# The second layer's keys and values, and the quantisation of the feed-forward weights, made in the experts' stage

## The chip, the cores and the metric

The kernel runs on one core of one Trainium2 chip. The metric is the device time of one execution in microseconds (us), the median of several runs.

## What is computed

Two layers with gates work on x, 64 sequences of 128 tokens by 256 numbers. Each layer has cross attention with 16 heads to a context (64 x 128 x 256), and then a feed-forward part. In the first layer that part is a mixture of 64 experts (each token goes to 8 of them, an expert takes 256 rows at most) with a shared expert. In the second it is a gated feed-forward with 704 inner columns whose activations and weights are quantised to 8 bits. Cut to what matters here:

```
for each layer L:
    q = norm(x) @ wq + bq;  k = ctx @ wk + bk;  v = ctx @ wv + bv      # ctx is the same in both layers
    x = x + tanh(g_xattn[L]) * (softmax(q k^T / 4, masked in L = 1) v @ wo + bo)
    x = x + tanh(g_ffn[L]) * ffn_L(norm(x))
ffn_0: route each token to 8 of 64 experts, silu(xe w1^T) * (xe w3^T) @ w2^T, weighted, added up; plus a shared expert
ffn_1: w_gate, w_up, w_down rounded to 127 steps of their rows' maxima; activations to 127 steps of one global maximum
```

Keys and values of the second layer depend on the context and the weights alone, not on what the first layer gives. So do the quantised weights.

## The kernel before

Each engine runs its own program, written out in full, and semaphores tie them. `phase_end` is a barrier of all five engines between stages. The stages are: constants; attention of layer 0 with routing and the shared expert (`attention_*(..., 0)`); the experts (`experts_*`); attention of layer 1 (`attention_*(..., 1)`); and two passes of the second feed-forward part.

**Slots.** A stage is a software pipeline. `slots` calls a `body` for slot s, and `stage(lag)` in it is batch (or expert) s - lag with its ring number, or nothing. In the attention of layer 1 the slot's letters are g = s + 1, f = s, m = s - 1, k = s - 2, o = s - 3, w = s - 4 and v = s - 5. Every engine works through its own body in order, so an instruction that waits holds all that stand behind it.

**A slot of layer 1.** TensorE: `scores(m)` into the four banks `tiles`, after mask matmuls (L336) that begin the same banks; `project_qk(f)` (L434) and `project_v(f)` (L449) from the context tile `cx`; masks and transposed scores `scores_t(k)` (L369); `heads_to_tokens(o)` (L480), `output(w)` (L469), `tokens_to_heads(o)` (L490), `transposes(g)` (L415), `maxima_t(m)` (L385), `values(k)` (L399). VectorE: `maximum(m)` (L810), `first_sum` of batch s + 2 (L852: the two halves `ax` of the first layer's result, loaded from the two accumulators in DRAM), `first_stats` (L862), `head_sums(o)` (L909), `head_norm(o)` (L918), `token_maximum`, `residual` (L835), statistics, `shifted(m)` (L822). ScalarE: two normalisations, `copy_qk(f)` (L621 queries, L624 keys in two masked forms), `copy_v(f)` (L634), the exponential (L601), three copies. The keys and values of the first three batches (`KV_FIRST`) are made at the end of the experts' stage, so those slots project queries alone.

**SyncE** issues the loads of layer 1 in `attention_sp`: in slot s, `load` for batch s + 3, first the context (L1090) after waits on the projections of four batches before, then the two `ax` loads (L1112) after a wait on `sum_done` of two batches before. The ring of `cx` has four tiles and that of `ax` two.

**Experts.** For each of 64 experts GpSimd gathers two blocks of 128 rows (L1442) two slots ahead and adds two blocks of results into an accumulator in DRAM (L1457); these are indirect DMAs. TensorE makes the map of rows (L1221), transposes the rows (L1234, ScalarE copies them, L1321), multiplies up (L1252) and down (L1270), and makes the router's logits (L1258). SyncE loads the weights of the expert four ahead.

**Quantisation.** `weights_dve` on VectorE, `weights_pe` and `weights_act` work at the end of the attention of layer 0, from about slot 61, in buffers that this stage no longer uses (`qkp`, `cxax`, `pt`). The main line L771 rounds one matrix of 128 x 1536. SyncE stores the result (L1504) behind the loads of the second layer's weights and the first experts' weights (L1180, L1181), and then ends the stage.

Of the kernel before, what the change touches and what calls it, by code (L numbers as in the profile page):

```python
# [5 lines left out]
def flamingo_gated_two_layers(nc: bass.Bass, a, out: bass.AP):  # L6
# [10 lines left out]
    P = 128  # L17
# [32 lines left out]
    KV_FIRST = 3  # L50
# [11 lines left out]
    hidden_away = nc.dram_tensor("hidden_away", [len(AWAY), P, IC * CT], f32).ap()  # L62
    ffn_int = nc.dram_tensor("ffn_int", [3, P, KC * IP], bf16).ap()

    ctx = ExitStack()
    with ctx:
# [147 lines left out]
        wraw = [qkp[:, 3 * n:3 * n + 3, :].rearrange("p a (c d) -> p (a c) d", d=D) for n in range(2)]  # L214
        wdraw = cxax[:, 0:6, :].rearrange("p a d -> p (a d)")[:, 0:KC * I].rearrange("p (k i) -> p k i", k=KC)
        wq_b = pt[1][:, 2:4, :].rearrange("p a d -> p (a d)").bitcast(bf16)[:, 0:KC * IP]
        ws = [w.rearrange("p a d -> p (a d)").bitcast(bf16)[:, 0:KC * IP] for w in (pt[0][:, 2:4, :], ovs[:, :, :], qkp[:, 0:2, :])]
# [78 lines left out]
        MADE_WEIGHTS = (8 if IREST else 6) * 2 + 11  # L296
# [26 lines left out]
        TILES_IN_0 = 8 * NB  # L323
# [3 lines left out]
        def attention_pe(pe, L):  # L327
            def sm(name):
                return f"{name}_{L}"

# [8 lines left out]
            def scores(m):  # L339
# [4 lines left out]
                wait(pe, sm("exp_done"), b - 1)  # L344
# [9 lines left out]
                last.then_inc(sem(sm("s_done")), 1)  # L354

            def scores_t(k):
# [4 lines left out]
                pe.wait_ge(sem(sm("max_done")), ahead(b, 2))  # L361
                if L == 1:
                    masks(1)
                pe.wait_ge(sem(sm("qm_done")), b + 1)
# [6 lines left out]
                last.then_inc(sem(sm("st_done")), 1)  # L371

            def maxima_t(m):
# [4 lines left out]
                pe.wait_ge(sem(sm("max_done")), b + 1)  # L378
# [6 lines left out]
                nc.tensor.transpose(bk[:, 0:P], mt[:, :], ident[:, :]).then_inc(sem(sm("mt_done")), 1)  # L385

            def values(k):
# [5 lines left out]
                pe.wait_ge(sem(sm("exp_done")), b + 1)  # L393
                pe.wait_ge(sem(sm("v_out")), b + 1)
                wait(pe, sm("at_out"), b)
# [5 lines left out]
                last.then_inc(sem(sm("pv_done")), 1)  # L401

            def transposes(f):
# [6 lines left out]
                if L == 0:  # L410
                    pe.wait_ge(sem(sm("v_out")), b + 1)
                else:
                    wait(pe, sm("v_out"), b)
# [4 lines left out]
            def project_qk(f):  # L418
# [5 lines left out]
                pe.wait_ge(sem(f"tile_in{r}"), (2 - L) * (4 * (b - r) + 16) + L * TILES_IN_0)  # L424
# [5 lines left out]
                for j in range(KC):  # L430
                    for n, w in enumerate((w_q, w_k)[:1 if L == 1 and b < KV_FIRST else 2]):
# [4 lines left out]
                last.then_inc(sem(sm("qk_done")), 1)  # L436
# [153 lines left out]
        def attention_act(act, L):  # L590
            def sm(name):
                return f"{name}_{L}"
# [1492 lines left out]
```

## Time and profile before

| | |
|---|---|
| median of 3 runs | 2064.66 us (2063.12 to 2065.77) |
| the profiled execution | 2069.3 us, its span 2067.5 us |
| TensorE matmul, busy | 1832.9 us, 89% |
| TensorE weight load | 1463.2 us, 71% |
| VectorE | 1402.3 us, 68% |
| ScalarE | 1119.8 us, 54% |
| GpSimd | 562.2 us, 27% |
| mean granted TensorE clock | 0.945 of 2.4 GHz |

The numbers are of one execution that the hardware profiler took. Times in the rows are us from the start of the span, unless they say ns. PE is TensorE's matmul and PEld its weight load, DVE is VectorE, ACT ScalarE, POOL GpSimd, SPq the queue of SyncE's DMA issues. `L434` is line 434 of the kernel. In a row of the timeline the first two numbers are start and duration, x16 are sixteen instructions merged, and brackets hold the idle time before it and what ended that. Ends of matmuls are modelled, and their durations overlap, so distances between starts are the surer figure.

### The profile page before, as it was taken

How to read it: one execution, taken by the hardware profiler on the slowest of the kernel's cores; microseconds unless marked ns; L12 is line 12 of the kernel's file. 1: busy time of each engine (PE TensorE's matmuls, PEld its weight loads, DVE VectorE, ACT ScalarE, POOL GpSimd, SP SyncE). 2: the span in 40 equal slices, each digit the busy share in tenths (PEclk: the TensorE clock that was granted, in tenths of full speed). 3: DMA queues.
4: the chain of work that ended last, by engine and by line, in shares of the span. 5: the costliest groups of instructions: out<-in, count | busy, mean ns of one | idle time of the engine just before them, and what ended most of it. 6: DMA issues, size and time to landing. Idle time of an engine off the chain costs nothing.

```text
span 2067.5 us, 55165 instructions
## 1 busy us (share of the span) xinstructions
PE 1832.9 (89%) x20966; PEld 1463.2 (71%) x20976; DVE 1402.3 (68%) x4715; ACT 1119.8 (54%) x2347; POOL 562.2 (27%) x551
## 2 busy tenths in 40 slices
PE   6999999999999994888778876999999999978855
PEld 4888888888888873666666664777777777753334
DVE  4778878787878776444444435666666666658988
ACT  3666666666666651111111124666666666658875
POOL 1000000000000001788888871111111111111147
PEclk9999999999999996888888888999999999999989
DMA  3122222222222215666666652111111111102355
GB/s 96 45 60 61 61 64 60 71 61 64 61 63 61 58 43 182 139 140 141 142 141 143 133 98 64 48 41 48 45 43 48 41 48 41 40 25 111 134 214 193
DMA packets 158646, 174.30 MB, mean 84 GB/s; under 512 B 22512, under 2 KB 142704, under 8 KB 156208
## 3 DMA queue, kind: packets, MB, share of 16 engines
q1 hardware_dynamic: 133568, 136.34, 21.9%
q0 software_dynamic: 24816, 34.42, 9.9%
q8 instruction: 170, 2.79, 0.6%
q14 instruction: 92, 0.75, 0.1%
HBM read 104.72 MB, written 65.98 MB: 83 GB/s over the span
## 4 chain that ended last, share of the span: by engine, by line
PE 66%; DVE 14%; issue 8%; POOL 5%; DMA 4%; ACT 2%; POOLq 0%; SPq 0%; DVEq 0%; ACTq 0%
PE bank L434 12%; PE tiles L369 7%; PE tiles L352 7%; PE bank L399 6%; PE bank L517 6%; PE bank L449 5%; PE bank L480 4%; PE bank L469 3%; PE bank L540 3%; PE tiles L1252 3%; DVE hmax L1660 2%; POOL accumulator L1457 2%; PE tiles L336 2%; POOL xr L1442 2%; DMA xr<-token_rows,tid 2%
## 5 line engine op out<-in xcount | busy, mean ns | idle before, releaser
L1920 POOL TENSOR_TENSOR rstd<-var,minus_half 128x2 f32<-128x2 f32 x138 | 96.1, 696 | 1142.9 <-DVE var L887 1142.7
L810 DVE TENSOR_REDUCE mt<-tiles 128x16 f32<-128x2048 f32 x128 | 293.5, 2293 | 113.6 <-PE tiles L352 113.6
L601 ACT ACTIVATE pt<-tiles 128x2048 f32<-128x2048 f32 x128 | 240.8, 1881 | 13.1 <-PE tiles L369 8.5
L1457 POOL DMA_INDIRECT accumulator<-ye,tid x128 | 205.0, 1601 | 42.8 <-issue 31.7
L624 ACT ACTIVATE qkp<-bank,kb,keep 128x128 f32<-128x128 f32 x500 | 205.2, 475 | 0.0
L1405 DVE TENSOR_SCALAR ye<-bank,wcol 128x256 f32<-128x256 f32 x128 | 56.0, 479 | 216.3 <-PE bank L1270 175.1
L434 PE MATMUL bank<-xt,w_q 128*128 128x128 f32 x1024 | 165.1, 285 | 0.9 <-ACT xt L609 0.9
L621 ACT ACTIVATE qkp<-bank,qb 128x128 f32<-128x128 f32 x256 | 96.0, 376 | 123.9 <-PE bank L434 123.7
L1442 POOL DMA_INDIRECT xr<-token_rows,tid x128 | 137.3, 1072 | 81.1 <-DVE within L1370 44.5
L434 PE MATMUL bank<-cxax,w_k 128*128 128x128 f32 x1000 | 154.3, 277 | 0.0
L434 PEld LDWEIGHTS bank<-xt,w_q 128*128 128x128 f32 x1024 | 136.8, 195 | 22.6 <-issue 20.9
L369 PE MATMUL tiles<-qm,qkp 32*128 32x128 f32 x4096 | 150.2, 283 | 1.4 <-DVE mt L810 1.4
L352 PE MATMUL tiles<-qkp 32*128 32x256 f32 x2048 | 148.1, 402 | 3.2 <-ACT qkp L624 3.2
L1321 ACT COPY xrt<-tiles 128x512 f32<-128x512 f32 x64 | 37.5, 586 | 206.6 <-PE tiles L1234 173.2
L369 PEld LDWEIGHTS tiles<-qm,qkp 32*128 32x128 f32 x4096 | 125.8, 186 | 27.2 <-issue 24.3
L399 PE MATMUL bank<-pt,vx 128*32 128x128 f32 x4096 | 138.4, 276 | 2.3 <-ACT pt L601 1.5
L434 PEld LDWEIGHTS bank<-cxax,w_k 128*128 128x128 f32 x1000 | 133.5, 194 | 0.0
L469 PE MATMUL bank<-w_o,at 128*128 128x256 f32 x512 | 131.8, 380 | 0.5 <-ACT at L676 0.5
L667 ACT COPY ovs<-bank 128x512 f32<-128x512 f32 x128 | 75.1, 587 | 102.2 <-PE bank L399 102.2
L449 PE MATMUL bank<-w_v,cxax 128*128 128x256 f32 x500 | 130.2, 383 | 0.0
L1234 PE MATMUL tiles<-ident,xr 128*128 128x128 f32 x256 | 53.0, 342 | 78.9 <-DMA xr<-token_rows,tid 78.9
L352 PEld LDWEIGHTS tiles<-qkp 32*128 32x128 f32 x2048 | 92.7, 185 | 34.9 <-issue 26.9
(255 smaller groups left out, 4079.3 us busy)
## 6 DMA issues: line engine op xcount, KB each, us to landing
cxax<-in_ctx SPq DMA_DIRECT2D x128, 128.0 KB, 2.6
cxax<-accumulator SPq DMA_DIRECT2D x128, 128.0 KB, 2.2
hidden_away<-h_ring SPq DMA_DIRECT2D x8, 1536.0 KB, 5.1
pt<-in_expert_up SPq DMA_DIRECT2D x36, 256.0 KB, 4.6
token_rows<-pay SPq DMA_DIRECT2D x64, 128.5 KB, 2.7
res<-in_x SPq DMA_DIRECT2D x64, 128.0 KB, 2.7
accumulator<-xa SPq DMA_DIRECT2D x64, 128.0 KB, 1.7
accumulator<-zt SPq DMA_DIRECT2D x64, 128.0 KB, 1.8
```

What stands on the lines that cost most here:

```text
L352: last = nc.tensor.matmul(both, qt[r % 2][rows, j, :], kp[r][rows, :, j, :], start=(L == 0), stop=True, skip_group_check=(L == 1))
L369: last = nc.tensor.matmul(tiles[:, i, n * P:(n + 1) * P], kp[r][rows, e, j, :], qm[rows, e, j, :], start=(L == 0), stop=True, skip_group_c ...
L399: last = nc.tensor.matmul(bank[7][32 * h:32 * h + 32, g * P:(g + 1) * P], vx[r][:, GH * g + h, :], pt[p][:, i, n * P:(n + 1) * P], start=T ...
L434: last = nc.tensor.matmul(o_, w[:, c, j * P:(j + 1) * P], (cx[r] if n else xt[p])[:, c, :], start=(c == 0), stop=(c == KC - 1))
L449: last = nc.tensor.matmul(bank[4][:, 0:D], cx[r][:, c, :], w_v[:, c, :], start=(c == 0), stop=(c == KC - 1))
L469: last = nc.tensor.matmul(bank[6][:, 0:D], at[r % 2][:, c, :], w_o[:, c, :], start=(L == 1 and c == 0), stop=(c == KC - 1))
L517: last = nc.tensor.matmul(bank[4][:, n * FS + j * P:n * FS + (j + 1) * P], w[:, c, j * P:(j + 1) * P], x2t[p][:, c, :], start=(c == 0), st ...
L601: nc.scalar.activation(pt[r % 2][:, :, :], tiles[:, :, :], ACT.Exp).then_inc(sem(sm("exp_done")), 1)
L624: last = nc.scalar.activation(kp[r][:, e, j, :], bank[5][:, (KC + j) * P:(KC + j + 1) * P], ACT.Identity, bias=kb[:, e, j:j + 1], scale=ke ...
L810: nc.vector.tensor_reduce(mt[:, :].rearrange("p (i n c) -> p i n c", i=RT, n=2 * KC)[:, :, :, 0], tiles[:, :, :].rearrange("p i (n k) -> p ...
L1442: nc.gpsimd.indirect_dma_start(out=xr[r][:, h, :], out_offset=None, in_=rows[:, :], in_offset=bass.IndirectOffsetOnAxis(ap=tid[n % 8][:, h ...
L1457: nc.gpsimd.indirect_dma_start(out=acc[p][:, :], out_offset=bass.IndirectOffsetOnAxis(ap=tid[b % 8][:, h:h + 1], axis=0), in_=ye[r][:, h, ...
```

## The change

Line numbers in front of functions are those of the kernel before. What it does:

- In the experts' stage TensorE gets `keys_or_values` between `rows_t` and `up`: for expert slot n, with n even, the keys of batches n and n + 1 (four matmuls of 256 columns), with n odd their values. ScalarE copies bank 5 to `kvs`, and SyncE stores it to a new DRAM tensor `keys_values` (256 KB for each slot). Pairs of context tiles are loaded four pairs ahead (`load_pair`). `rows_t` uses one PSUM bank in place of two.
- In the attention of layer 1 `project_v` and the key half of `project_qk` are gone, and so is the load of the context. `copy_qk` and `copy_v` read keys and values from `kvt`, a ring of two in SBUF. `load` fills it from `keys_values` with two DMAs, and these stand in front of the `ax` loads.
- `first_keys_values_*` and `KV_FIRST` are gone.
- The quantisation gets room of its own in rows 8 to 55 of `res` (free once batch 55 of the first layer is stored). Its loads, and the first four pairs of context, are issued in the slot of the first attention in which batch 56 is stored. VectorE does one step of it in each of the experts' slots from 3 on; TensorE transposes in slots 8, 9, 13, 14, 20, 21 and 23; SyncE stores the results in slots 11, 16 and 23.
- Semaphores of the two layers' attention are counted on over both (`first = L * NB`), which frees some of them and changes no wait otherwise.

```diff
@@ buffers
-        wraw = [qkp[:, 3 * n:3 * n + 3, :].rearrange("p a (c d) -> p (a c) d", d=D) for n in range(2)]
...
+        wraw = [room(8 + 6 * n, 6).rearrange("p (c d) -> p c d", d=D) for n in range(2)]
+        wdraw = room(20, 6)[:, 0:KC * I].rearrange("p (k i) -> p k i", k=KC)
+        wq_b = [room(26 + 3 * n, 3).bitcast(bf16)[:, 0:KC * IP] for n in range(3)]
+        ws = [room(35 + 3 * n, 3).bitcast(bf16)[:, 0:KC * IP] for n in range(3)]
+        cxp = [room(44 + 2 * k, 2).rearrange("p (c e t) -> p c e t", c=KC, e=2) for k in range(4)]
+        kvs = [room(52 + 2 * k, 2) for k in range(2)]
+        ROOM_FROM, ROOM_TO = 8, 56
+        kvt = [cxax[:, 2 * k:2 * k + 2, :].rearrange("p a d -> p (a d)") for k in range(2)]
@@ attention_pe, body of layer 1
                     project_qk(f)
-                    project_v(f)
                     scores_t(k)
@@ attention_act, copy_qk and copy_v
+                if L == 1:
+                    act.wait_ge(sem(f"kv_in{p}"), 16 * (b - p) + 32)
...
+                    k = bank[5][:, (KC + j) * P:(KC + j + 1) * P] if L == 0 else kvt[p][:, j * P:(j + 1) * P]
+                    for e in range(2):
+                        last = nc.scalar.activation(kp[r][:, e, j, :], k, ACT.Identity, bias=kb[:, e, j:j + 1], scale=keep[:, e:e + 1])
...
+                v = bank[4][:, 0:D] if L == 0 else kvt[p][:, D:2 * D]
@@ attention_sp, load
-                if L == 0 or b >= KV_FIRST:
-                    wait(sp, sm("v_done"), b - 3)
-                    wait(sp, sm("qk_done"), b - 3)
+                if L == 0:
+                    wait(sp, "v_done", first + b - 3)
+                    wait(sp, "qk_done", first + b - 3)
                     load_context(sp, b, r)
-                if L == 0:
                     sp.dma_start(res[:, bass.ds(b, 1), :].rearrange("p o d -> p (o d)"),
...
                 else:
+                    wait(sp, sm("qk_out"), 2 * (b - 1))
+                    wait(sp, sm("v_out"), b - 1)
+                    sp.dma_start(kvt[p][:, 0:D].rearrange("p (c t) -> p c t", c=KC),
+                                 keys_values[b - p].rearrange("p (c e t) -> p c e t", c=KC, e=2)[:, :, p, :]).then_inc(sem(f"kv_in{p}"), 16)
+                    sp.dma_start(kvt[p][:, D:2 * D], keys_values[b - p + 1][:, p * D:(p + 1) * D]).then_inc(sem(f"kv_in{p}"), 16)
                     wait(sp, sm("sum_done"), b - 1)
                     for n_ in range(2):
                         sp.dma_start(ax[p][:, n_, :], acc[n_][bass.ds(b * P, P), :]).then_inc(sem(f"ax_in{p}"), 16)
@@ attention_sp, body of layer 0
-                    if stage(5) is not None and stage(5)[0] == NB - 2:
+                    if stage(5) is not None and stage(5)[0] == ROOM_TO:
                         ffn_weights_in(sp)
@@ experts_sp
+            def keep_pair(e):
+                if e is None:
+                    return
+                n, r = e
+                p = r % 2
+                sp.wait_ge(sem("kv_out"), n + 1)
+                sp.dma_start(keys_values[n], kvs[p]).then_inc(sem(f"kv_kept{p}"), 16)
+                if p == 1 and n // 2 + 4 < PAIRS:
+                    load_pair(sp, n // 2 + 4)
+
             def body(stage):
                 load_weights(stage(0))
+                keep_pair(stage(1))
+                if stage(0) is not None and stage(0)[0] in WEIGHTS_OUT_AT:
+                    ffn_weights_out(sp, WEIGHTS_OUT_AT[stage(0)[0]])
@@ experts_pe
+            def keys_or_values(e):
+                if e is None:
+                    return
+                n, _ = e
+                j = n // 2
+                if n == 0:
+                    pe.wait_ge(sem("w_in"), 16 * 16)
+                pe.wait_ge(sem(f"pair_in{j % 4}"), 8 * (j - j % 4) + 32)
+                wait(pe, "kv_out", n)
+                for k in range(2):
+                    for c in range(KC):
+                        if n % 2 == 0:
+                            weights_, moving = w_k[:, c, k * P:(k + 1) * P], cxp[j % 4][:, c, :, :].rearrange("p e t -> p (e t)")
+                        else:
+                            weights_, moving = cxp[j % 4][:, c, k, :], w_v[:, c, :]
+                        last = nc.tensor.matmul(bank[5][:, k * D:(k + 1) * D], weights_, moving, start=(c == 0), stop=(c == KC - 1))
+                last.then_inc(sem("kv_done"), 1)
@@ experts_act
+            def copy_pair(e):
...
+                act.wait_ge(sem("kv_done"), n + 1)
+                wait(act, f"kv_kept{p}", 8 * (n - p))
+                nc.scalar.copy(kvs[p], bank[5][:, :]).then_inc(sem("kv_out"), 1)
@@ experts_dve, body
                 hidden(stage(1))
+                if stage(0) is not None and stage(0)[0] > 2 and stage(0)[0] != E // 4 and stage(0)[0] != E // 4 + 4:
+                    next(weights, None)
                 next_layer(stage(0))
@@ the program of SyncE
             sp.wait_ge(sem("pv_done"), NB)
             first_expert_weights(sp)
-            ffn_weights_out(sp)
```

## Rows read from the trace of the kernel before

**Rows 1.** Busy time by stage: stretch, its length, each engine's busy, PEclk, DMA share, GB/s
```profile
749.00:809.00 60.00, 32.80 (x312) 26.01 (x310) 47.35 (x196) 16.56 (x34) 2.07 (x3) 0.79 0.45 145
809.00:1246.00 437.00, 344.57 (x1705) 281.83 (x1705) 191.65 (x873) 78.36 (x207) 342.24 (x256) 0.83 0.65 132
1246.00:1850.00 604.00, 578.66 (x9230) 435.82 (x9230) 398.43 (x893) 397.77 (x814) 94.04 (x132) 0.99 0.15 45
```

**Rows 2.** Timeline, one slot of the second attention: start, duration, engine, line
```profile
1502.94 0.71 PE L434 MATMUL bank<-xt,w_q 128*128 128x128 f32 x4
1503.08 2.29 DVE L810 TENSOR_REDUCE mt<-tiles 128x16 f32<-128x2048 f32 x1 [1.04 <-PE tiles L352]
...
1505.03 0.37 ACT L621 ACTIVATE qkp<-bank,qb 128x128 f32<-128x128 f32 x1 [1.82 <-PE bank L434]
1505.29 0.41 DVE L852 TENSOR_TENSOR res<-cxax 128x256 f32<-128x256 f32 x1
...
1505.79 0.43 PE L336 MATMUL tiles<-mask_bias,identb 32*32 32x512 bf16 x16
...
1506.92 0.40 ACT L634 COPY vx<-bank 128x256 f32<-128x256 f32 x1
...
1507.75 1.03 PE L469 MATMUL bank<-w_o,at 128*128 128x256 f32 x4
1508.24 0.42 DVE L918 TENSOR_TENSOR on<-bank,rden 128x256 f32<-128x256 f32 x1
...
1508.72 0.44 PE L490 MATMUL bank<-ident,on 128*128 128x128 f32 x2
...
1510.77 0.43 PE L336 MATMUL tiles<-mask_bias,identb 32*32 32x512 bf16 x16
...
1512.21 0.71 PE L434 MATMUL bank<-xt,w_q 128*128 128x128 f32 x4
```

**Rows 3.** Timeline, the stage's end: mask matmuls of slots without projections
```profile
1835.40 0.43 PE L336 MATMUL tiles<-mask_bias,identb 32*32 32x512 bf16 x16
...
1844.32 0.43 PE L336 MATMUL tiles<-mask_bias,identb 32*32 32x512 bf16 x16
```

**Rows 4.** Timeline, the stage's first loads and the sum that waits for them
```profile
1246.43 3.91 SPq L1112 DMA_DIRECT2D cxax<-accumulator  x6
1249.09 0.42 DVE L852 TENSOR_TENSOR res<-cxax 128x256 f32<-128x256 f32 x1 [14.86 <-DMA cxax<-accumulator]
```

**Rows 5.** Timeline, the first slots, with queries alone: at the low clock, then the full
```profile
1253.43 2.08 PE L434 MATMUL bank<-xt,w_q 128*128 128x128 f32 x8 [0.46 <-ACT xt L609]
...
1255.86 0.65 PE L336 MATMUL tiles<-mask_bias,identb 32*32 32x512 bf16 x16
...
1258.12 1.16 PE L434 MATMUL bank<-xt,w_q 128*128 128x128 f32 x8
...
1259.32 0.63 ACT L621 ACTIVATE qkp<-bank,qb 128x128 f32<-128x128 f32 x2 [2.28 <-PE bank L434]
```

**Rows 6.** Busy time in the experts' stage: a gap of TensorE, and what follows
```profile
1028.10:1031.00 2.90, 0.00 (x0) 0.00 (x0) 2.74 (x14) 0.00 (x0) 2.29 (x3) 0.66 0.72 205
1031.00:1036.00 5.00, 4.96 (x17) 4.25 (x17) 0.10 (x1) 0.97 (x2) 4.08 (x4) 0.51 0.56 93
```

**Rows 7.** Timeline, the first attention's end: quantisation and SyncE's last issues
```profile
782.12 1.75 DVE L761 TENSOR_REDUCE s_gu<-qkp 128x6 f32<-128x1536 f32 x1
...
790.61 0.96 DVE L771 TENSOR_SCALAR qkp<-qkp 128x1536 f32<-128x1536 f32 x1
...
802.14 0.43 SPq L1181 DMA_DIRECT2D xt<-in_L_ffn_w  x1
...
809.13 1.79 SPq L1844 DMA_DIRECT2D res<-in_mask_1x1xSxS_ik  x4
```

**Rows 8.** GpSimd's indirect DMAs, one line each: ns min/median/max, first and last start
```profile
L1442 POOL DMA_INDIRECT xr<-token_rows,tid x128: 1012/1061/1157, 812.8 to 1218.1; - x128
L1457 POOL DMA_INDIRECT accumulator<-ye,tid x128: 1557/1592/1851, 831.2 to 1238.0; - x128
```

## Prediction of the time

> **What bounds the kernel now.** I read the busy times by stage first. There are four stages that matter here: the first layer's attention with routing up to 749 us, its tail to 809, the experts to 1246, the second attention to 1850 [rows 1]. The change touches the last three. In the second attention TensorE is busy 579 of 604 us, VectorE and ScalarE two thirds of it: the reader would say that TensorE is the bound and that taking matmuls away pays one for one. In the experts' stage the figures to see are TensorE's 345 of 437 us at a granted clock of 0.83 and the DMA share of 0.65.
>
> The second view is one slot of the second attention in order of time [rows 2]. A slot is 9.27 us (L434 at 1502.94 and again at 1512.21). Inside it one group of PSUM banks, `tiles`, is written by the scores, read by the maximum (L810, 2.29 us), written again by the transposed scores, and read by the exponential. Of L434 and L449, the projections of queries, keys and values, all but the queries leave; they run while the maximum runs. So their time is not the slot's time. The trace has slots without any projection, at the end of the stage: from mask matmul to mask matmul 8.92 us [rows 3]. That is the floor that the change can reach with everything else as it is: 0.35 us less per slot, although it takes 1.77 us of matmuls away (the eight key matmuls about 0.9, the values 0.87; L469, of the same form as the values, is 1.03 with its overlap).
>
> **Second attention: what is put in.** Eight matmuls of keys and four of values go, and with them one load of context in each slot. In come two loads, of keys and of values, into two buffers (`kvt`), each read by ScalarE in the place of PSUM (the same count of activations, priced the same). What matters is the order on SyncE. In `load`, batch b's key and value loads wait for `qk_out_1` and `v_out_1` of batch b-2, since there are two buffers. Behind them, in the same queue, stand the two loads of the accumulators (`ax`) of batch b. Before, `ax` stood behind a wait on batch b-4's projection, so two slots early. VectorE needs `ax` of batch b in `first_sum`, right behind the maximum, in slot b-2: the very slot in which ScalarE copies the values of batch b-2. Everything behind `first_sum` on VectorE waits with it: `head_sums`, `head_norm`, the residual, the shifted queries. For `head_norm` waits TensorE (L490), in order, and behind that stand the values' matmuls and the next slot's scores, whose projection ScalarE's next copy waits for. It is a closed loop of one slot.
>
> I walk it from L434 = 0, with the distances of [rows 2], and of other rows where the slot changes:
> - queries alone to ScalarE's first copy: 1.20 (1258.12 to 1259.32, where only queries are projected [rows 5]), in place of 2.09
> - ScalarE's first copy to the end of the copy of values (1505.03 to 1507.32): 2.29, together 3.49
> - two issues for keys and values at 0.43 and a small gap [rows 7]: 0.95, together 4.44
> - first issue of `ax` to `first_sum`: 2.66 (1246.43 to 1249.09, where the DMA alone sets it [rows 4]), together 7.10; before it starts at 2.35
> - `first_sum` and `first_stats` 0.85, reciprocal and `head_norm` 0.71 (L918 ends at 1508.66): together 8.66
> - `head_norm`'s end to the next mask matmul (1510.77): 2.11, and to the next L434 (1512.21) 1.44: **12.21 us** for a slot, 2.94 more.
>
> **The clock.** In this new slot TensorE ends L469 about 5.5 us after L434 (the maximum ends at 2.43, then 3.0 of work as from 1505.79 to 1508.78 [rows 2]) and waits for L490 till 8.7: 3.2 us idle in every slot. Before there is no such gap and the clock is 0.99 [rows 1]. What a gap of that length does stands in the experts' stage: 2.9 us without a matmul, the clock falls to 0.5 and the next 5 us run at 0.51, the 1.2 GHz level [rows 6]. Five gaps of 2.6 to 3.1 us between 1028 and 1100 all show it, with 2.5 to 5 us of work at the low level behind each; of two gaps of 2.2 (at 1008) and 2.3 us (at 1837) the first does, for 7.9. What it costs on the path: full queries 2.08 against 1.16, and mask to queries 2.26 (1255.86 to 1258.12) against 1.44 [rows 2, 5]. All of the path after the gap at the low level is 0.8 + 0.9 + about 1.3 for the maxima's transpose and the values + 0.7 where L490 and L415 outgrow VectorE's cover, 3.7 us. I take 4.4 us of the low level after a gap, the mean of those six, half of it lost: 2.2. **Slot 14.4 us**, between 12.2 and 15.9.
>
> Slots 3 to 61 pay it (batches 2 to 63 are loaded this way): 59 x 5.1 = 303. The three first slots are short now, and pay about 3 each; the first `ax` starts 0.9 behind two new issues. Sum **+313** for the stage.
>
> **Tail of the first stage.** The quantisation ran on VectorE there, and its last store is what SyncE waits for: the experts' stage begins at 809.13. Without it SyncE's last issue is the expert weights' at 802.14, and these come about 1.8 us earlier, since L761 and its small steps (782.12, 1.75 us and more) no longer stand between routing steps. **-8 us**, bounds -6 to -10 [rows 7]. The weights' 5 loads and 8 of context now come in one slot of the first attention: 13 issues at 0.47 are 6 us on a queue that has about 7 issues in a slot of 11.6 us, and the next user of each buffer is two slots away. I take 0; it could be 3.
>
> **Experts' stage.** Here GpSimd makes the descriptors: 2 x 1.06 and 2 x 1.59 us and four gaps of 0.3, 6.5 us for each of 64 experts, 437 us in all [rows 1, 8]. It is the bound. TensorE gets 64 x 0.87 us (four matmuls of 256 columns): 345 + 56 is 401, up to 61 more at the granted clock, 406 of 437: it fits, and its gaps get shorter, which speaks for a higher clock. ScalarE gets 64 copies of 512 columns and VectorE some 17 us in 20 slots, at 192 of 437: cover enough. The DMA engines are the tight one: 384 KB more per expert is 58 GB/s beside 132, at the row's own ratio 0.28 more share, 0.93. Each gather, each add and each weight load still has a slot or more of slack. I take **+4**, with 0 and +25 as ends (the upper is a tenth of a slot per expert with one stalled slot in five). If the cover were gone, TensorE's part is worth 56 us.
>
> The quantisation's `tensor_scalar` of 1536 elements takes 0.96 us [rows 7], beside GpSimd's descriptors in the new place; gathers vary by 0.1 and adds by 0.3 us about their medians [rows 8], with short VectorE work beside them. The Trainium skill (SBUF — State Buffer, "Who interferes with whom") says that VectorE's single-input SBUF operations in their two-port mode and GpSimd lock each other out of a shared port pair for a whole instruction. By that rule, which speaks against this move, six such operations would delay the bound engine by at most 5.7 us; the sum above takes nothing for it and its upper end holds it.
>
> **Sum.** -8 + 4 + 313 = +309. The profiled execution took 2069.3 us (span 2067.5), so it becomes 2378; it lies 4.6 above the median of the runs, and for the median I say **2374**.
>
> **Rivals.**
> - The loop closes, but the clock stays up: slots of 12.2 us, 59 x 2.94 = 173, and 10 - 8 + 4: 2244. For it: one gap of 2.3 us did no harm. Against: five of five over 2.6 did.
> - The loop closes and all the path runs at the low level: 59 x 6.6 = 390, in all +396: 2461. For it: the fall comes anew in every slot. Against: no work behind a gap stayed low for over 8 us.
> - The experts' stage turns to TensorE or DMA: a tenth longer, +45 in place of +4: 2415. For it the share of 0.93; against, that the added work shortens the idle time that lowers the clock.
> - Faster: the `ax` loads land before VectorE needs them. Then TensorE's projections are gone, slots fall to the floor of 8.92, 62 x 0.35 = 22, and with -8 and +4 the time is 2039. It decides at `first_sum` starting less than 2.4 us after L434, that is if `ax` could be issued ahead of the copies of batch b-2. The order of the queue says that it can't.
>
> **How the numbers follow.** Forecast 0.53, full clock 0.20, low clock 0.09, longer experts' stage 0.11, faster 0.06, and 0.01 for no change. The range reaches from a little below the full-clock case to a little above the low one, 2225 to 2470, which leaves about 0.15 out. A measurement of this kernel tells a change from none at about 0.2%. Faster 0.06, same 0.01, slower 0.93.
>
> **What would show it.** After the change `first_sum` (the sum of the two `ax` halves) waits for a DMA in each slot of the second attention, some 3.5 to 5 us; TensorE's longest idle is ahead of the transposes of `on` and is put down to VectorE; the stage's slots are 12 to 16 us and its clock 0.75 to 0.9. The experts' stage keeps 6.4 to 6.6 us per expert and GpSimd has next to no idle time. The experts begin near 801. If slots are at 9 us or less, the queue argument is wrong; if GpSimd waits for `ye` or for its own adds, the experts' term is.

## The result, and the profile after the change

The changed kernel takes 2378.88 us (median of four runs, 2372.41 to 2381.23), the kernel before 2065.22 us in the same comparison: a ratio of 1.150 (95% interval 1.148 to 1.152). The prediction was 2374. The profiled execution took 2380.58 us, its span 2378.8.

| | before | after | difference | predicted |
|---|---|---|---|---|
| the experts' first gather | 812.8 | 800.6 | -12.2 | -8 |
| from there to the second attention's first load | 433.6 | 443.8 | +10.1 | +4 |
| from there to the first maximum over all tokens | 612.5 | 927.9 | +315.4 | +313 |
| the rest | 208.5 | 206.6 | -1.9 | 0 |

Busy time of the changed kernel by stage, to be laid beside [rows 1] (stretch, its length; busy time of PE, PEld, DVE, ACT and POOL; granted clock, DMA share, GB/s): the tail of the first attention, the experts, the second attention.

```profile
737.00:797.00 60.00, 35.20 (x365) 29.06 (x364) 33.68 (x188) 16.89 (x40) 2.75 (x4) 0.85 0.25 77
797.00:1244.00 447.00, 399.19 (x2219) 336.84 (x2218) 209.17 (x900) 115.22 (x262) 347.64 (x256) 0.96 0.81 187
1244.00:2172.00 928.00, 581.55 (x8512) 410.56 (x8512) 402.63 (x910) 423.18 (x832) 95.27 (x134) 0.85 0.13 39
```

In the second attention TensorE was busy in 96% of the time before and is in 63% now, at a clock of 0.85. No other engine has taken its place: VectorE and ScalarE are under 46%, DMA at 0.13. A stage in which nobody is busy is bound by a chain of waits. The costliest groups name it (busy, mean ns | idle before, releaser):

```profile
L497 PE MATMUL bank<-ident,on 128*128 128x128 f32 x256 | 65.8, 345 | 233.2 <-DVE on L933 233.2
L867 DVE TENSOR_TENSOR res<-cxax 128x256 f32<-128x256 f32 x64 | 27.2, 425 | 355.6 <-DMA cxax<-accumulator 355.6
L688 ACT COPY at<-bank 128x256 f32<-128x256 f32 x128 | 47.6, 372 | 316.7 <-PE bank L497 316.7
```

ScalarE (L688) waits for TensorE (L497), TensorE for VectorE (L933), and VectorE for a DMA: `first_sum` (now L867) waits 355.6 us for `ax`, 5.6 in each of 63 slots. One slot shows where that DMA was (start, duration, engine, line, idle time before it and what ended that):

```profile
1512.61 1.20 PE L444 MATMUL bank<-xt,w_q 128*128 128x128 f32 x8
...
1513.85 0.37 ACT L630 ACTIVATE qkp<-bank,qb 128x128 f32<-128x128 f32 x1 [2.13 <-PE bank L444]
...
1515.89 0.40 ACT L647 COPY vx<-cxax 128x256 f32<-128x256 f32 x1
1516.36 0.52 SPq L1122 DMA_DIRECT2D cxax<-keys_values  x1
...
1516.93 0.80 SPq L1124 DMA_DIRECT2D cxax<-keys_values  x1
...
1517.78 0.91 SPq L1127 DMA_DIRECT2D cxax<-accumulator  x2
1520.69 0.42 DVE L867 TENSOR_TENSOR res<-cxax 128x256 f32<-128x256 f32 x1 [5.65 <-DMA cxax<-accumulator]
...
1521.77 0.42 DVE L933 TENSOR_TENSOR on<-bank,rden 128x256 f32<-128x256 f32 x1
...
1522.24 0.44 PE L497 MATMUL bank<-ident,on 128*128 128x128 f32 x2 [4.15 <-DVE on L933]
...
1523.43 1.94 PE L408 MATMUL bank<-pt,vx 128*32 128x128 f32 x32
...
1525.29 0.65 PE L345 MATMUL tiles<-mask_bias,identb 32*32 32x512 bf16 x16
...
1527.17 0.60 PE L444 MATMUL bank<-xt,w_q 128*128 128x128 f32 x3
```

The copy of the values (L647) ends at 1516.29, and SyncE issues the next key load (L1122) at 1516.36: it stood waiting for that copy. The `ax` loads (L1127) come third, at 1517.78, and land when VectorE has waited 5.65 us. The group of projections starts 14.56 us apart here. As a mean over 61 slots (from the third `first_sum` to the last) a slot takes 9.14 us before and 14.13 after; the medians are 9.27 and 14.15, since the first slots are short in both.

### The profile page after: what moved, and what is told of

Read it like the earlier page. It is cut to its first block, busy times and chain, and to the rows that moved or that the text cites. A ratio compares the mean times of both kernels' runs of the same rounds, so it can differ in the third digit from the quotient of the medians.

```text
span 2378.8 us, 55048 instructions
## 1 busy us (share of the span) xinstructions
PE 1876.1 (79%) x20710; PEld 1483.4 (62%) x20720; DVE 1400.3 (59%) x4713; ACT 1174.4 (49%) x2411; POOL 567.2 (24%) x551
## 3 DMA queue, kind: packets, MB, share of 16 engines
q8 instruction: 168, 2.75, 0.5%
## 4 chain that ended last, share of the span: by engine, by line
PE 57%; DVE 13%; DMA 10%; ACT 7%; issue 6%; SPq 5%; POOL 2%; POOLq 0%; ACTq 0%; DVEq 0%
PE bank L444 8%; PE bank L408 7%; PE tiles L361 6%; DMA cxax<-accumulator 6%; PE bank L524 5%; ACT qkp L633 4%; PE tiles L378 3%; DMA xr<-token_rows,tid 3%; PE bank L1268 3%; PE tiles L1300 2%; PE bank L476 2%; PE bank L547 2%; PE bank L456 2%; PE bank L497 2%; DVE hmax L1709 2%
## 5 line engine op out<-in xcount | busy, mean ns | idle before, releaser
L497 PE MATMUL bank<-ident,on 128*128 128x128 f32 x256 | 65.8, 345 | 233.2 <-DVE on L933 233.2
L867 DVE TENSOR_TENSOR res<-cxax 128x256 f32<-128x256 f32 x64 | 27.2, 425 | 355.6 <-DMA cxax<-accumulator 355.6
L688 ACT COPY at<-bank 128x256 f32<-128x256 f32 x128 | 47.6, 372 | 316.7 <-PE bank L497 316.7
L497 PEld LDWEIGHTS bank<-ident,on 128*128 128x128 f32 x256 | 29.0, 159 | 266.3 <-DVE on L933 258.7
L408 PE MATMUL bank<-pt,vx 128*32 128x128 f32 x4096 | 188.4, 342 | 1.8 <-ACT pt L608 1.2
L361 PE MATMUL tiles<-qkp 32*128 32x256 f32 x2048 | 166.5, 442 | 3.6 <-ACT qkp L633 3.5
L444 PE MATMUL bank<-xt,w_q 128*128 128x128 f32 x1024 | 155.7, 286 | 0.9 <-ACT xt L616 0.9
L408 PEld LDWEIGHTS bank<-pt,vx 128*32 128x32 f32 x4096 | 138.3, 137 | 28.2 <-issue 15.1
L345 PE MATMUL tiles<-mask_bias,identb 32*32 32x512 bf16 x2048 | 64.8, 456 | 86.5 <-DVE mt L825 86.5
L361 PEld LDWEIGHTS tiles<-qkp 32*128 32x128 f32 x2048 | 103.5, 209 | 46.3 <-issue 34.8
```

Source lines behind the costliest of these rows:

```text
L361: last = nc.tensor.matmul(both, qt[r % 2][rows, j, :], kp[r][rows, :, j, :], start=(L == 0), stop=True, skip_group_check=(L == 1))
L408: last = nc.tensor.matmul(bank[7][32 * h:32 * h + 32, g * P:(g + 1) * P], vx[r][:, GH * g + h, :], pt[p][:, i, n * P:(n + 1) * P], start=T ...
L444: last = nc.tensor.matmul(o_, w[:, c, j * P:(j + 1) * P], (cx[r] if n else xt[p])[:, c, :], start=(c == 0), stop=(c == KC - 1))
L497: last = nc.tensor.transpose(bank[7][:, c * P:(c + 1) * P], on[r % 2][:, c * P:(c + 1) * P], ident[:, :])
```

## The experiments

My theory is the prediction's: the slot is a closed loop from ScalarE's copies over SyncE's queue to `first_sum` in the same slot, and the clock falls in the gap that this makes. "Slot" below is the mean that was just defined. Where a time has no interval beside it, it is that of a single run; the four runs of the changed kernel lie within 9 us of each other.

**The order in SyncE's queue.** The two accumulator loads moved in front:

```diff
+                    wait(sp, sm("sum_done"), b - 1)
+                    for n_ in range(2):
+                        sp.dma_start(ax[p][:, n_, :], acc[n_][bass.ds(b * P, P), :])...
                     wait(sp, sm("qk_out"), 2 * (b - 1))
                     wait(sp, sm("v_out"), b - 1)
...
-                    wait(sp, sm("sum_done"), b - 1)
-                    for n_ in range(2):
-                        sp.dma_start(ax[p][:, n_, :], acc[n_][bass.ds(b * P, P), :])...
```

> Only the order of the four loads of a slot in the second attention is changed: the two accumulator loads stand in front of the two of keys and values, with the same waits. Theory (the accumulator loads are held behind the copies of keys and values): first_sum waits for nothing, slots fall from 14.1 us to the floor of 8.9 that the kernel before shows without projections, TensorE's gap of 4.2 us goes and with it the low clock; 62 x 5.2 = 322 less, about 2055 us. Rival (the two added loads cost by themselves, their traffic or SyncE's time): the slots stay above 12 us and the time above 2250. Rival (TensorE is still the bound and all of the projections' 1.77 us comes off): slots of 7.5 us, 1970.

Measured: 2050.54 us, a ratio to the kernel before of 0.993 (0.990 to 0.995). A slot takes 8.86 us, the granted clock is 1.00 in the middle of the stage and the waits of `first_sum` for DMA shrink from 355.6 to 16.1 us. In a slot of it `first_sum` starts 2.35 us after the projection, and waits for nothing:

```profile
1504.65 1.16 PE L444 MATMUL bank<-xt,w_q 128*128 128x128 f32 x8
...
1507.00 0.41 DVE L867 TENSOR_TENSOR res<-cxax 128x256 f32<-128x256 f32 x1
...
1507.14 0.44 PE L345 MATMUL tiles<-mask_bias,identb 32*32 32x512 bf16 x16 [1.33 <-DVE mt L825]
```

No transfer and no instruction was taken away, so neither the added loads nor ScalarE's reads from SBUF cost the 328 us: their place in the queue did.

The same from the other side: the order stays, but the ring for keys and values has four tiles.

```diff
-        kvt = [cxax[:, 2 * k:2 * k + 2, :]... for k in range(2)]
+        kvt = [cxax[:, 2 * k:2 * k + 2, :]... for k in range(2)] + [w[:, :, :]... for w in (w_k, w_v)]
-                    wait(sp, sm("qk_out"), 2 * (b - 1))
-                    wait(sp, sm("v_out"), b - 1)
+                    wait(sp, sm("qk_out"), 2 * (b - 3))
+                    wait(sp, sm("v_out"), b - 3)
```

(`kvt` and its semaphores are then counted by the ring of four.)

> The changed kernel, order of SyncE's queue untouched (keys and values still in front of the accumulators' loads), but the ring for keys and values has four tiles in place of two (the other two are the weights w_k and w_v, idle in this stage), so their loads wait for the copies of four batches before. If the wait on the copies of two batches before closes the loop, it is open here too: slots of 8.9 us and a total as with the accumulators' loads in front, 2050 +-8. If instead it is the position of two more issues ahead of the accumulators' loads that costs, slots stay above 13 us and the total above 2300.

Measured: 2050.55 us, 0.992 (0.990 to 0.994), a slot of 8.80. So the accumulators' loads may stand third in the queue, if what stands in front of them needn't wait. It is the wait in front of the loads, for a copy of two batches before in a ring of two, that closes the loop.

What an issue in front of them costs, with the loop closed: the values' load is taken away (and ScalarE's waits count one load for each batch in place of two), so this kernel leaves out the values of the second layer.

```diff
-                    sp.dma_start(kvt[p][:, D:2 * D], keys_values[b - p + 1]...)
```

> The changed kernel without the load of the values in the second attention (the values read there are old data; the rest is done in full). Theory (each issue that stands in front of the accumulator loads is in the loop): one issue of 0.6 us and its gap off each slot, 13.5 in place of 14.1, 62 x 0.65 = 40 less, 2340. Rival (the wait for the copies is all of it, issues overlap): 2380. Rival (the loads' traffic delays the accumulators' landing): over 1 us a slot, below 2315.

Measured: 2355.62 us, a slot of 13.73: 0.40 less in each, 23 in all, where the issue and its gap are 0.65. At the median the first `ax` issue follows the copy of the values after 0.65 us in place of 1.28, and the sum follows that issue after 2.89 in place of 2.81. So the loop runs through the issues, and the slot keeps part of each one's price.

**The clock.** Filler matmuls between the output projection and the transposes of `on`, in every slot, twelve and then six:

```diff
+                    if o is not None and f is not None:
+                        pe.wait_ge(sem(sm("qk_out")), 2 * (f[0] + 1))
+                    for n_ in range(12 if o is not None and f is not None else 0):
+                        nc.tensor.matmul(bank[5][:, D:2 * D], w_k[:, n_ % 2, 0:P], w_v[:, n_ % 2, :], start=True, stop=True)
```

> The changed kernel with twelve matmuls of 256 columns more in each slot (2.6 us, results unused), where TensorE waits for head_norm, so that the gap of 4.2 us shrinks below 2. The loop through the loads is as before. Theory (a loop of some 13.1 us and 1 to 1.5 us more by the low clock): the clock of the stage goes from 0.86 to 0.97 or more, a slot from 14.1 to 12.9 to 13.1 us, the time down by 60 to 75 us to about 2310, although work was added. Rival (the clock costs nothing, the loop alone sets 14.1): no change, 2380. Rival (the added matmuls lie on the path): 2.6 us more in each slot, 2540.

Measured: 2369.77 us, a slot of 13.70. The size was wrong: such a matmul is recorded as two and takes about 0.45 us, where I had taken 0.22, so the twelve ran 5.3 us and ended about 1 us after `on` was there. The clock in the middle of the stage was 1.00, and most of the gain went into the overshoot. So this run gives no price; the next one does.

> As the kernel with twelve filler matmuls, but with six in each slot (about 2.6 us), so that they end before the normalised heads are there. It prices the clock: the same loop with TensorE kept busy. By my prediction's step the low clock costs 2.2 us in each slot, so 60 slots give 130 less: about 2250. By the reading of the slots after the change (two stretches of the path grew by 1.0 and 0.4 us against the full clock) it costs 1.0 to 1.4: slots of 13.0, 60 to 85 less in all, 2295 to 2320. If the clock costs nothing: 2380.

Measured: 2328.18 us, 51 less than the changed kernel; the slot 13.14, at a clock of 0.98 in the middle of the stage (0.86 in the changed kernel). One slot of it:

```profile
1503.43 1.16 PE L444 MATMUL bank<-xt,w_q 128*128 128x128 f32 x8
...
1504.63 0.37 ACT L634 ACTIVATE qkp<-bank,qb 128x128 f32<-128x128 f32 x1 [0.93 <-PE bank L444]
...
1506.68 0.39 ACT L651 COPY vx<-cxax 128x256 f32<-128x256 f32 x1
...
1508.36 0.91 SPq L1131 DMA_DIRECT2D cxax<-accumulator  x2
...
1508.75 2.75 PE L591 MATMUL bank<-w_v,w_k 128*128 128x256 f32 x12
1511.28 0.42 DVE L871 TENSOR_TENSOR res<-cxax 128x256 f32<-128x256 f32 x1 [5.41 <-DMA cxax<-accumulator]
...
1512.35 0.42 DVE L937 TENSOR_TENSOR on<-bank,rden 128x256 f32<-128x256 f32 x1
...
1512.83 0.44 PE L497 MATMUL bank<-ident,on 128*128 128x128 f32 x2 [1.33 <-DVE on L937]
...
1514.88 0.43 PE L345 MATMUL tiles<-mask_bias,identb 32*32 32x512 bf16 x16
...
1516.32 0.94 PE L444 MATMUL bank<-xt,w_q 128*128 128x128 f32 x6
```

At the full level the loop takes 12.89 us here (1503.43 to 1516.32; the median of all slots is 12.98). `first_sum` still waits 5.41. The low level costs 1.0 us of the mean slot (14.13 against 13.14), not 2.2, and 1.2 of the median one. The cost falls where the gap has just ended: from `on` to the masks 2.11 us here, 3.10 in the changed kernel, and from there to the projection 1.44 against 1.88.

**The experts' stage.** I measure it from the start of the first gather to that of the last add, both on GpSimd: 425.2 and 424.8 us in the two kernels with the old stage, 432.7 to 435.3 (mean 433.8) in nine with the new one, so +8.8. First, the three products and the three roundings of the quantisation cut to an eighth of their columns (most of each weight matrix is left unrounded):

```diff
-                st.then(V.tensor_tensor(wraw[n], wraw[n], inv[...].unsqueeze(2).broadcast_to([P, IC, D]), ALU.mult))
+                st.then(V.tensor_tensor(wraw[n][:, :, 0:32], wraw[n][:, :, 0:32], inv[...].unsqueeze(2).broadcast_to([P, IC, 32]), ALU.mult))
```

> The changed kernel with six of VectorE's quantisation instructions (the three products and the three roundings) cut to an eighth of their columns, so that the weights are quantised for a part only; count and order of instructions are unchanged. Theory (these instructions hold GpSimd, whose gathers of 1.06 us took 2.2 to 2.5 beside the products): the longest gather falls from 2.54 to under 1.3 us, the experts' stage shortens by 4 to 6 us of its 447.5. Rival (the stage is 10 us longer than before because of TensorE and DMA): it stays within 1 us.

Measured: a stretch of 430.2 us, 3.6 under that mean and 5.1 under the changed kernel; the total, 2382.61, doesn't show it, since the experts began at 807.6 there and at 800.6 in the changed kernel, which scatters. The trace of the changed kernel shows how VectorE's work reaches GpSimd:

```profile
840.40 1.75 DVE L777 TENSOR_TENSOR res<-res,inv 128x1536 f32<-128x1536 f32 x1
840.84 2.24 POOL L1481 DMA_INDIRECT xr<-token_rows,tid  x1 [0.31 <-issue]
...
845.31 2.15 POOL L1496 DMA_INDIRECT accumulator<-ye,tid  x1 [0.30 <-issue]
846.42 0.95 DVE L779 TENSOR_SCALAR res<-res 128x1536 f32<-128x1536 f32 x1
...
L1481 POOL DMA_INDIRECT xr<-token_rows,tid x128: 1007/1060/2538, 800.6 to 1215.6; - x128
L1496 POOL DMA_INDIRECT accumulator<-ye,tid x128: 1557/1598/2147, 822.5 to 1235.8; - x128
```

A gather takes 1.06 us at the median and 2.24 beside the product. The three products, each with both inputs in SBUF, lengthen three gathers by 1.2, 1.5 and 1.3 us; single-input operations of the quantisation lengthen three of the five adds that they meet by 0.35 to 0.55 us. Before, the longest gather was 1.16 us [rows 8]. With the cut, the longest gather and add take 1.75 and 1.73; that gather stands beside L781, a single-input operation which the cut leaves whole.

Second, the new transfers cut to an eighth. This kernel leaves out most of the keys and values, and its second attention loads parts of the context of the same size in their place:

```diff
-                sp.dma_start(keys_values[n], kvs[p]).then_inc(...)
+                sp.dma_start(keys_values[n][:, 0:64], kvs[p][:, 0:64]).then_inc(...)
-                sp.dma_start(cxp[j % 4][:, :, e, :], a["ctx_1024"]...)
+                sp.dma_start(cxp[j % 4][:, :, e, 0:16], a["ctx_1024"][..., 0:16]...)
```

> The changed kernel, with the new transfers of the experts' stage cut to an eighth (an eighth of each pair of contexts loaded, an eighth of keys and values stored), as many DMAs, matmuls and copies as there; the second attention loads parts of the context of the same size in place of its keys and values. From the first gather to the end of the last add: 427 us before, 437 after, 432 with the quantisation cut. If traffic is what is left of the 10 us, the stretch is 432 here too; if it is in the descriptors' own time and in the fill, it stays at 436 to 437. The DMA share falls from 0.86 to about 0.7 in either case, and the total is within 6 us of the changed kernel's.

Measured: the stretch 432.3 us at a DMA share of 0.72 in place of 0.85. That is 1.5 under the mean of the nine, and hardly outside their spread, so traffic is little of the 8.8, if any. The total was 2354.55, 24 less, which I had not expected: the slot of the second attention is 13.74. The two loads read the context there, in another layout, and their issues take 0.38 and 0.47 us at the median and not 0.52 and 0.60; the first `ax` issue follows the copy after 1.01 us in place of 1.28, and the sum follows it after 2.74 in place of 2.81. By the medians that is 0.34 of the 0.4 us that a slot lost.

GpSimd's own times split the 10.1 us between the two profiled kernels. Its gathers and adds last 342.2 us before [rows 1] and 347.6 after (the second row by stage above), 5.4 more, and 343.3 with the quantisation cut. Its idle times of over 0.6 us sum to 7.8 us before and 12.6 after, and these 4.7 are the rest; the short gaps between its instructions are 76.6 us in both.

Most of that rest stands at the stage's start. From first gather to first add it takes 18.4 us in the kernel before (18.6 in the other one with the old stage) and 21.9 in the changed one, and 21.1 to 22.4 in ten others with the new stage, the two cuts among them. In the changed kernel these stand before the first down projection (L1318), and L1268 is new:

```profile
805.86 3.62 PE L1268 MATMUL bank<-res,w_k 128*128 128x256 f32 x8
...
810.25 1.96 PE L1268 MATMUL bank<-w_v,res 128*128 128x256 f32 x8
812.05 1.89 PE L1300 MATMUL tiles<-xrt,wlast 128*128 128x256 f32 x8
...
815.36 1.89 PE L1268 MATMUL bank<-res,w_k 128*128 128x256 f32 x8
...
819.63 1.11 PE L1318 MATMUL bank<-wlast,he 128*128 128x256 f32 x4
```

While the pipeline fills, TensorE's work is the path, and three groups of the new matmuls are in it. That this is the cause of the 3.5 us is read, not tried.

**What taking the projections out is worth.** With the loop open the slot fell by 0.3 us only, though 1.77 us of matmuls had gone. In the kernel with the accumulators' loads in front TensorE waits 1.33 us for the maximum. Two work items moved into that wait:

```diff
                     project_qk(f)
-                    scores_t(k)
                     heads_to_tokens(o)
                     output(w)
+                    scores_t(k)
```

> The kernel with the accumulators' loads in front, and TensorE's order in the second attention changed: the transposes of the raw heads and the output projection stand before the transposed scores, in the 1.33 us in which TensorE waits for the maximum. If TensorE is still the bound there, the slot loses that wait whole: 7.6 us, 1970. If the loop through the banks of the scores holds it (scores 1.6, maximum 2.3, transposed scores 1.6, exponential 1.9, and the values' matmuls 1.1 behind it, in order), the slot is 8.6: about 0.3 less, 2030 +-8.

Measured: 2052.78 us (0.993, 0.991 to 0.995), nothing gained, a slot of 8.80. The wait for the maximum is gone, and TensorE waits 1.38 us ahead of the values' matmuls instead:

```profile
1508.11 1.88 ACT L608 ACTIVATE pt<-tiles 128x2048 f32<-128x2048 f32 x1 [0.45 <-PE tiles L378]
...
1509.88 0.37 ACT L688 COPY at<-bank 128x256 f32<-128x256 f32 x1
...
1510.40 1.08 PE L408 MATMUL bank<-pt,vx 128*32 128x128 f32 x32 [1.38 <-ACT at L688]
1511.41 0.43 PE L345 MATMUL tiles<-mask_bias,identb 32*32 32x512 bf16 x16
```

Neither expectation was right to the number: I had left out that the values' matmuls write a bank that ScalarE reads first (L688), and that this copy stands behind the exponential. So the values' matmuls moved out of the loop, behind the next slot's scores (`output` stands behind the transposed scores again):

```diff
                     # TensorE, against the kernel with the accumulators' loads in front
+                    values(o)
                     project_qk(f)
+                    heads_to_tokens(o)
                     scores_t(k)
-                    heads_to_tokens(o)
                     output(w)
                     tokens_to_heads(o)
                     transposes(g)
                     maxima_t(m)
-                    values(k)
                     # ScalarE
+                    copy_ov(o)
                     copy_qk(f)
-                    copy_v(f)
                     exponent(k)
+                    copy_v(f)
                     copy_at(o)
                     copy_xt(g)
-                    copy_ov(k)
```

> As the last, with the values' matmuls of a batch moved behind the next slot's scores (and ScalarE's copy of their result with them, its copy of the loaded values behind the exponential), so that they run during the maximum and not between the exponential and the next scores. If the loop through the banks of the scores is what holds the slot, it becomes 7.6 to 7.9 us, so 60 x 1.0 to 1.3 less than with the accumulators' loads in front alone: 1975 to 1995. If ScalarE (7.3 us of work in a slot) or a chain through it takes over: 8.3 to 8.9, 2015 to 2050.

Measured: 1984.36 us, 0.961 (0.959 to 0.962), a slot of 7.82. The loop through the banks of the scores was what held it. The same two orders in the kernel before, where the projections stay (ScalarE's copy of the values keeps its place ahead of the exponential there, since the next transposes need its bank; in this one point the orders differ):

```diff
                     # TensorE
+                    values(o)
                     project_qk(f)
                     project_v(f)
+                    heads_to_tokens(o)
                     scores_t(k)
-                    heads_to_tokens(o)
...
-                    values(k)
                     # ScalarE
+                    copy_ov(o)
...
-                    copy_ov(k)
```

> The kernel before (all projections in the second attention), with the same two reorderings of that stage as in the run with the values' matmuls behind the next scores. It tells what taking the projections out is worth once the loop through the banks of the scores is short. With TensorE's whole work in a slot (7.6 us there, and 1.77 of keys and values) it can't fall under 9.3 us, what it has: 2060 to 2075, no gain. If the reordering alone brought the 66 us, and the projections were still hidden, it would come near 1995.

Measured: 2069.50 us, 1.000 (0.999 to 1.002), a slot of 9.13. The orders alone bring nothing, the change with its queue mended brings 0.7%, and both together 3.9%. Last, both with four buffers as well, that is, the edits of the runs with `ax` in front, with four tiles and with the values late in one kernel:

> The kernel with the values' matmuls late, and four buffers for keys and values as well. In the former first_sum still waits 0.9 to 1.1 us in 53 slots for its loads, since they queue on SyncE behind the wait for the copy of values, which now comes after the exponential. If that wait holds the slot (7.62 us), it becomes 7.4 or so, and the total 1968 to 1978. If TensorE holds it (377 of 400 us busy there), the wait was beside it: 1984 +-4.

Measured: 1970.07 us, 0.952 (0.950 to 0.954): the fastest. The slot is 7.57; `first_sum`, which still waited for DMA 53 times with two buffers (73.8 us), does so once, at the stage's start:

```profile
1506.86 0.42 DVE L867 TENSOR_TENSOR res<-cxax 128x256 f32<-128x256 f32 x1
1507.05 0.14 PEld L345 LDWEIGHTS tiles<-mask_bias,identb 32*32 32x32 bf16 x16 [0.16 <-DVE mt L825]
...
1507.31 0.79 SPq L1122 DMA_DIRECT2D cxax<-accumulator  x2
...
1508.78 1.86 ACT L608 ACTIVATE pt<-tiles 128x2048 f32<-128x2048 f32 x1
...
1510.69 0.14 PEld L345 LDWEIGHTS tiles<-mask_bias,identb 32*32 32x32 bf16 x16 [0.26 <-ACT pt L608]
```

The slot is full: the next masks follow 1.9 us after the exponential's start (1508.78), TensorE's waits shown are 0.2 and 0.3 us, and it is busy in 384 of the 400 us from 1300 on. Against the kernel before with the same orders it is 99 us less, 1.56 in each slot: nearly the 1.77 us of matmuls one for one.

## Why the prediction was right, point by point

- **The closed loop** is shown from both sides: open it by the order or by two more buffers, and 328 us go. It was read off the order of one queue and the lengths of two rings.
- **Its length at the full level** was 12.21; it is 12.89. The copies end 0.15 later, mostly since two of ScalarE's key copies take 0.87 us from SBUF and took 0.80 to 0.82 from PSUM, as two rows of the kernel before show, in the slot of [rows 2]:

```profile
1505.30 0.80 ACT L624 ACTIVATE qkp<-bank,kb,keep 128x128 f32<-128x128 f32 x2
...
1506.23 0.82 ACT L624 ACTIVATE qkp<-bank,kb,keep 128x128 f32<-128x128 f32 x2
```

  The two issues and their gaps take 1.29 and not 0.95: I had priced them at 0.43, from a load of weights [rows 7], and these take 0.52 and 0.60. From the first `ax` issue to the sum it is 2.92, not 2.66. With -0.07 for the rest that makes 0.68. The wait of `first_sum` was accordingly 5.6 us a slot, above the 3.5 to 5 that I had named as its sign, and TensorE's gap 3.9 at the median and not 3.2.
- **The clock** I had at 2.2 us a slot; it costs 1.0 to 1.2. I had taken half of 4.4 us of low level as lost. Its length was about right: a clock of 0.86 in slots of 14.15 us is an estimate of 4.0 us at half the clock in each. Wrong was the half, which was about a quarter; I read that the rest lay beside VectorE's part of the loop or in the wait for the maximum, and no run separates the two. The two errors, +0.7 and -1.0, nearly cancelled: slot 14.4 predicted and 14.13 found. That 313 was met so closely is therefore in part luck. By place the sum fits: 304 of the 315 us lie between the third and the last `first_sum`, where I had 303, and 10 before the third, where I had 10. The clock of 0.85 in the stage lies inside the 0.75 to 0.9 named.
- **The experts' beginning**: -8 predicted, -12.2 in the profiled pair. Over all profiles (eleven at 800.6 to 807.6, mean 804.0, and two at 812.8 and 813.2) it is -9.1.
- **The experts' stage**: +4 predicted, within 0 to 25, and +8.8 to +10 found. GpSimd stays the bound (6.56 us an expert from the first add to the last, within the 6.4 to 6.6 named) and TensorE fits. The DMA share became 0.81, where I had worked out 0.93. But two terms were mis-sized. The new matmuls: four of 256 columns are eight in the trace, and cost 127 us and not 56 in all (66.7 and 60.6 for L1268); I read the +3.5 at the stage's start as their part. And I took nothing for what VectorE does to GpSimd's descriptors, where it is 3.6 to 5. The Trainium skill (SBUF — State Buffer, "Who interferes with whom") gives more than the one rule that I weighed: it says too that a VectorE instruction with both inputs in SBUF contends with a GpSimd instruction that reads SBUF. The trace agrees, and that half was the dearer one: 1.2 to 1.5 us for each of three gathers beside a product, against 0.35 to 0.55 for three adds beside a single-input operation.
- **The rivals.** Full clock (2244) falls: even held up by fillers the kernel takes 2328, since the loop itself was longer. All low (2461) and a longer experts' stage (2415) fall by the profile. The faster one decided at the point it named: with `ax` issued ahead, 2050.5 where I had worked out 2039.
- **The floor** of 8.92 us a slot, from the stage's last slots [rows 3], was right for the given order (8.86 and 8.80). It was a floor of the order and not of the work: 7.57 with another.

## What to carry to other kernels

Where a DMA queue serves two consumers, ask of each load what its wait is for and who stands behind it: here a wait on a copy of the same slot, put ahead of loads that had been two slots early, cost 15%, and either a swap of two blocks or two more buffers takes all of that back. Work taken off a busy engine is worth its time only if no loop through shared banks is as long: 1.77 us of matmuls brought 0.3 us, until one consumer was moved out of that loop, and then 1.3, and 1.56 with four buffers as well. Check the order of the work and the removal of work together, since here neither alone brought more than 0.8%, and both 4.8%.

## What the runs showed of the hardware that I had not expected

- A float32 matmul of the program is two matmuls in the trace, of 0.22 us each at 256 columns: twelve of the program ran 5.3 us, six 2.75.
- GpSimd's gathers lasted up to 2.54 us, 2.4 times their median, beside VectorE's products of two SBUF inputs of 1408 or 1536 elements.
- With more matmul work in the experts' stage its clock rose, from 0.83 to 0.98 between 850 and 1200 us (0.99 with the transfers cut). The up-projections of the experts (L1252 before, L1300 after) took 121 us in place of 157 in the whole stage, and the added 127 us of matmuls raised TensorE's busy time from 345 to 399 us only.
- A gap of about 4 us in every slot, and the low level after it, cost only 1.0 to 1.2 us of clock in each slot: the queries of the next slot are mostly at the full level again (a median of 1.16 us for their eight matmuls, as much as at the full level).
